# Two token-wise layers on one core: five parts of the instruction order regrouped around an in-order pipeline

## The reference

```python
# x: (2, 2048, 512), float32; per batch entry one expert of 5 and one category of 64
s0 = relu(x @ swi[0]) @ swo[0];  s1 = relu(x @ swi[1]) @ swo[1]     # 512 -> 2048 -> 512
eo = relu(x @ wi[type_label]) @ wo[type_label]
gate_in = concatenate([eo[:, 0], s0[:, 0], s1[:, 0]])               # first token only
w = softmax(relu(gate_in @ g1) @ g2)                                # 3 weights per batch entry
x = x + eo * w[0] + s0 * w[1] + s1 * w[2]
x = x + (x @ W[category] + b[category])
```

## Time and profile before

| | before |
|---|---|
| median of 3 runs | 2095.21 us (2089.08 to 2104.32) |
| profiled execution | 2096.13 us, span 2094.4 us |
| mean granted PE clock | 0.972 |
| PE busy | 1976.0 us (94% of the span), 8504 matmuls |
| DVE, ACT, POOL busy | 1258.6 (60%), 972.5 (46%), 857.7 us (41%) |
| chain that ended last | PE 84%, DMA 5%, issue 5%, DVE 4% |

### The profile page before, as it was taken

The page is one execution under the profiler, slowest core; times in us unless marked ns, Lnnn a source line. Parts: engine busy times, 40 slices in busy tenths (PEclk is TensorE's granted clock), DMA queues, the critical chain, the costliest instruction groups (busy, mean ns, idle before and its releaser), DMA issues.

```text
span 2094.4 us, 24883 instructions
## 1 busy us (share of the span) xinstructions
PE 1976.0 (94%) x8504; PEld 1618.5 (77%) x8504; DVE 1258.6 (60%) x1186; ACT 972.5 (46%) x1441; POOL 857.7 (41%) x607
## 2 busy tenths in 40 slices
PE   7999999888999898999899999988979989989998
PEld 5778777676788787888788888877868878878886
DVE  6778787778655454545644554576774645455545
ACT  5655755555553343334443444455554533334432
POOL 5767757557222232233422222365653222323233
PEclk8999999999999999999999999999999999999999
DMA  5666657656686575556686676576657756656653
GB/s 216 237 239 265 244 221 276 249 198 241 226 258 211 174 233 179 183 190 198 201 263 192 204 228 199 196 268 229 241 198 261 241 189 211 209 165 194 197 166 121
DMA packets 187024, 450.98 MB, mean 215 GB/s; under 512 B 16916, under 2 KB 57876, under 8 KB 180500
## 3 DMA queue, kind: packets, MB, share of 16 engines
q1 hardware_dynamic: 186900, 449.39, 63.4%
HBM read 308.81 MB, written 140.51 MB: 215 GB/s over the span
## 4 chain that ended last, share of the span: by engine, by line
PE 84%; DMA 5%; issue 5%; DVE 4%; ACT 1%; POOL 1%; SPq 0%; POOLq 0%; ACTq 0%; DVEq 0%
PE rps L1250 40%; PE ups L1250 40%; PE aps L1250 3%; DMA PDR<-in_L_cond_wo_dram 2%; DMA MB<-sums_kept 1%; DVE WD L953 1%; DMA XT<-in_x_dram 1%; DMA G1c<-in_L_cond_g_dram 1%; DVE WU L946 1%; DVE ACC L980 1%; DVE HL L963 1%; DVE XL L937 0%; POOL XT L660 0%; DMA PDR<-in_L_cond_swo_dram 0%; DVE gacc L1027 0%
## 5 line engine op out<-in xcount | busy, mean ns | idle before, releaser
L1250 PE MATMUL ups<-XH,WU 128*128 128x512 f32 x2688 | 901.0, 396 | 69.1 <-DVE HT L1002 25.7
L1250 PE MATMUL rps<-HH,WD 128*128 128x512 f32 x2688 | 898.5, 396 | 43.4 <-issue 42.5
L610 POOL TENSOR_TENSOR HT<-hid 128x512 f32<-128x512 f32 x192 | 267.4, 1393 | 1026.2 <-PE rps L1250 884.6
L1250 PEld LDWEIGHTS ups<-XH,WU 128*128 128x128 f32 x2688 | 513.3, 191 | 187.7 <-DVE HT L1002 27.4
L1250 PEld LDWEIGHTS rps<-HH,WD 128*128 128x128 f32 x2688 | 514.6, 191 | 159.4 <-issue 49.4
L1250 PE MATMUL rps<-HL,WD 128*128 128x512 f32 x1344 | 531.1, 395 | 0.0
L1250 PE MATMUL ups<-XL,WU 128*128 128x512 f32 x1344 | 530.3, 395 | 0.0
L963 DVE TENSOR_TENSOR HL<-HT,HH 128x1024 fp32r<-128x1024 f32 x240 | 305.9, 1294 | 47.7 <-POOL HT L610 35.0
L983 DVE SCALAR_TENSOR_TENSOR ACC<-rps,gw,ACC 128x1024 f32<-128x1024 f32 x129 | 165.4, 1283 | 277.7 <-PE rps L1250 277.7
L1250 PEld LDWEIGHTS rps<-HL,WD 128*128 128x128 f32 x1344 | 257.7, 192 | 53.8
L1250 PEld LDWEIGHTS ups<-XL,WU 128*128 128x128 f32 x1344 | 256.8, 191 | 52.7
(11 more groups left out here) (102 smaller groups left out, 1476.4 us busy)
## 6 DMA issues: line engine op xcount, KB each, us to landing
WU<-wu_kept SPq DMA_DIRECT2D x448, 256.0 KB, 3.2
WD<-wd_kept SPq DMA_DIRECT2D x224, 512.0 KB, 3.3
wd_kept<-WD SPq DMA_DIRECT2D x112, 512.0 KB, 2.9
wu_kept<-WU SPq DMA_DIRECT2D x32, 1024.0 KB, 5.8
wu_kept<-WU SPq DMA_DIRECT2D x32, 768.0 KB, 3.3
sums_kept<-ACC SPq DMA_DIRECT2D x28, 512.0 KB, 5.0
MB<-sums_kept SPq DMA_DIRECT2D x28, 512.0 KB, 5.6
PUR<-in_L_cond_swi_dram SPq DMA_DIRECT2D x16, 512.0 KB, 7.0
```

Source lines behind the costliest of these rows:

```text
L610: pool.tensor_tensor(dst, p, q, op).then_inc(s_T, 1)
L1250: ins = pe.matmul(dst, stationary[a], moving[c], start=start and j == 0, stop=stop and j == 2, skip_group_check=True)
```

## The change: what it does, and its diff

1. Weight requests: the down operand that was made after product 3 (product 0 of the next step) is made after product 4, together with product 1 (`made_after`). The raw down blocks of the next step are requested at i == 2, when product 5's low part is made; POOL's sums wait for product 6's low part.
2. Finishing of tokens: `mix(1, 2)` goes behind `second(6)`, and for odd c its load is requested at i == 5.
3. Ends of token blocks: `load_tokens(s + 1, 3)` is issued at the head of i == 5 instead of at i == 6; in the step `start` (rel 11) the low parts of token sums 2 and 3 come ahead of `hidden_low(d, 6)`.
4. Gate sums: the four operations of networks 0 and 1 are placed one by one in `second(1)` to `second(4)` of steps rel 8 and rel 9; those of the expert two by two in `second(0)` and `second(1)` of the gating step. The rest of the gate moves back by about two groups on PE, ACT and DVE. The second load of g1 is requested at i == 6.
5. First token sums: `XT` 4 and `XT` 5 of super 0 are made by POOL, beside DVE; their count moves to a semaphore of its own, and token sum semaphores are split in two. Super 0's low parts are awaited in the order in which they are made, and `up_low(0, 1)` comes before that of token block 2.
6. Hidden sums of half b: POOL makes HT 5 before HT 4, so HL 1 and HL 2 wait for three sums, not four.

The diff, without the hunks that only renumber semaphore counts:

```diff
+def made_after(m, i):
...
+    if i < 0:
+        m, i = m - 1, i + PRODUCTS
+    e = down_of(m, i) + WD_SLOTS
+    made = {PRODUCTS - WD_SLOTS: [], PRODUCTS - WD_SLOTS + 1: [e - 1, e]}.get(i, [e])
+    return [k for k in made if k >= 0 and prepared(k // PRODUCTS)]
...
+def x_low_count(s, i):
+    return PRODUCTS * s + (i if s == 0 else X_LO.index(i)) + 1
...
-s_xT = sem("token_sums")
+s_xT = sem("token_sums_T3_T2")
+s_xU = sem("token_sums_T1_T4")
...
         if PREP[N] >= 1:
-            sp.wait_ge(s_wld, PRODUCTS * PREP[N])
+            sp.wait_ge(s_wld, PRODUCTS * PREP[N] - 1)
+            sp.wait_ge(s_Sd, 4 * PREP[N])
...
         for i in range(PRODUCTS):
+            if i == 5 and m >= 0 and rel == STEPS_SUPER - 2 and s < SUPERS - 1:
+                load_tokens(s + 1, 3)
...
                         spill(d, j)
-            if e - 1 >= 0 and prepared((e - 1) // PRODUCTS):
-                keep_down((e - 1) // PRODUCTS, (e - 1) % PRODUCTS)
-            if i == 3 and prepared(N) and N > 0:
+            for k in made_after(m, i - 1):
+                keep_down(k // PRODUCTS, k % PRODUCTS)
+            if i == 2 and prepared(N) and N > 0:
...
                     if ms % 2 == 0:
-                        if stage == 0 and i in (2, 6):
+                        if stage == 0 and i == (5 if c % 2 else 2):
...
                             mix_tokens(ms, c + 1)
-                if s % 2 == 0 and i == 2:
-                    if rel == 7:
-                        load_g1(s // 2, 0)
-                    if rel == 8:
-                        load_g1(s // 2, 1)
+                if s % 2 == 0 and i == 2 and rel == 7:
+                    load_g1(s // 2, 0)
+                if s % 2 == 0 and i == 6 and rel == 8:
+                    load_g1(s // 2, 1)
...
                         load_tokens(s + 1, j)
-                if rel == STEPS_SUPER - 2 and i == 6 and s < SUPERS - 1:
-                    load_tokens(s + 1, 3)
...
         eng.wait_ge(s_xs[0], 16 * (s + 1))
-        eng.wait_ge(s_xT, 4 * s + 1)
+        eng.wait_ge(s_xT, 2 * s + 1)
...
     elif which == 2:
+        eng.wait_ge(s_xs[0], 16 * (s + 1))
+        eng.wait_ge(s_xs[1], 16 * (s + 1))
...
         eng.wait_ge(s_xs[3], 16 * (s + 1))
-        eng.wait_ge(s_xT, 4 * s + 2)
+        eng.wait_ge(s_xT, 2 * s + 2)
         dst, p, q, op = XT[:, 5, :], XT[:, 3, :], XT[:, 2, :], ALU.subtract
-    eng.tensor_tensor(dst, p, q, op).then_inc(s_xT, 1)
...
-x_from = [(XS, 0, 0, 0), (XT, 1, 1, 2), (XT, 2, 2, 4), (XT, 3, 0, 4), (XT, 4, 3, 0), (XT, 5, 4, 0), (XS, 2, 0, 0)]
+    eng.tensor_tensor(dst, p, q, op).then_inc(s_xT if which < 2 else s_xU, 1)
...
+none = (None, 0)
+x_from = [(XS, 0, none, none), (XT, 1, (s_xT, 1), (s_xT, 2)), (XT, 2, (s_xT, 2), (s_xU, 2)),
+          (XT, 3, none, (s_xU, 2)), (XT, 4, (s_xU, 1), none), (XT, 5, (s_xU, 2), none), (XS, 2, none, none)]
...
         pool.wait_ge(s_pd, 16 * (PREP[N] + 1))
+        if PREP[N] > 0:
+            pool.wait_ge(s_wld, PRODUCTS * PREP[N])
...
     up_sums(0)
+    token_sum(pool, 0, 2)
+    token_sum(pool, 0, 3)
...
         if d >= 0:
-            for which in range(4):
+            for which in (0, 1, 3, 2):
...
             act.wait_ge(s_up, PRODUCTS * (2 * STEPS_SUPER * s - 1) + i + 1)
-        t, slot, sums, _ = x_from[i]
-        if sums:
-            act.wait_ge(s_xT, 4 * s + sums)
+        t, slot, (made, count), _ = x_from[i]
+        if count:
+            act.wait_ge(made, 2 * s + count)
...
         if N > 0:
-            act.wait_ge(s_T, 8 * (N - 1) + 4 * half + 3)
+            act.wait_ge(s_T, 8 * (N - 1) + 5 * half + 3)
...
             else:
-                act.wait_ge(s_T, 8 * N + 4 + {3: 1, 2: 2, 4: 3, 5: 4}[i])
+                act.wait_ge(s_T, 8 * N + 4 + {3: 1, 2: 2, 5: 3, 4: 4}[i])
...
                 begin_sum(d, i)
-            e = down_of(m, i) + WD_SLOTS
-            if e >= 0 and prepared(e // PRODUCTS):
+            for e in made_after(m, i):
...
             chain(a)
-        if gating:
-            act.wait_ge(s_gps, 2 * (s // 2) + 1)
-            act.activation(gt[:, :], aps[:, 0:KD], ACT.Relu).then_inc(s_grelu, 1)
...
         second(2)
...
         second(2)
-        if gating:
-            act.wait_ge(s_gch, 2 * (s // 2) + 2)
-            act.activation(gexp[:, :], aps[:, 0:NETS], ACT.Exp,
...
         second(3)
+        if gating:
+            act.wait_ge(s_gps, 2 * (s // 2) + 1)
+            act.activation(gt[:, :], aps[:, 0:KD], ACT.Relu).then_inc(s_grelu, 1)
...
             relu_12(b)
+        if gating:
+            act.wait_ge(s_gch, 2 * (s // 2) + 2)
+            act.activation(gexp[:, :], aps[:, 0:NETS], ACT.Exp,
+                           bias=nmax[:, 0:1], accum_out=gsum[:, 0:1]).then_inc(s_gexp, 1)
+        if more:
...
         dve.wait_ge(s_xhi, PRODUCTS * s + X_HI.index(i) + 1)
-        t, slot, _, after = x_from[i]
-        if after:
-            dve.wait_ge(s_xT, 4 * s + after)
+        t, slot, _, (read, count) = x_from[i]
+        if count:
+            dve.wait_ge(read, 2 * s + count)
...
         dve.wait_ge(s_hhi, PRODUCTS * N + HI_ORDER.index(i) + 1)
-        after = {1: 8, 2: 8, 3: 6}
+        after = {1: 7, 2: 7, 3: 6}
...
-    def gate_partial(b, net):
+    def gate_partial(b, net, j):
...
-        for j in range(KD):
...
     token_low(0, 1)
-    token_sum(dve, 0, 2)
-    token_sum(dve, 0, 3)
-    token_low(0, 2)
...
                 add_sum(d, i)
-            e = down_of(m, i) + WD_SLOTS
-            if e >= 0 and prepared(e // PRODUCTS):
+            for e in made_after(m, i):
                 down_low(e // PRODUCTS, e % PRODUCTS)
+            if gating and i < 2:
+                gate_partial(s // 2, 2, 2 * i)
+                gate_partial(s // 2, 2, 2 * i + 1)
+            if m >= 0 and s % 2 == 0 and rel in (8, 9) and 1 <= i <= KD:
+                gate_partial(s // 2, rel - 8, i - 1)
...
             first_token(super_of(d - 1) // 2, net_of(d - 1))
-        if gating:
-            gate_partial(s // 2, 2)
         if m == -1:
-            for i in (3, 4, 5, 6):
+            for i in (2, 3, 4, 5, 6):
                 token_low(0, i)
-        if d >= 0:
-            hidden_low(d, 6)
...
             token_low(s + 1, 3)
+        if d >= 0:
+            hidden_low(d, 6)
...
         second(0)
-        if gating:
-            gate_terms(s // 2)
...
         second(2)
-        if gating:
-            gate_max(s // 2)
...
             up_low(b, 1)
+        second(3)
         if gating:
-            gate_weights(s // 2)
-        second(3)
+            gate_terms(s // 2)
...
         second(5)
-        mix(1, 2)
+        if gating:
+            gate_max(s // 2)
...
         second(6)
-        if m >= 0 and s % 2 == 0:
-            if rel == 7:
-                gate_partial(s // 2, 0)
-            if rel == 8:
-                gate_partial(s // 2, 1)
+        mix(1, 2)
+        if gating:
+            gate_weights(s // 2)
...
         if n % (2 * STEPS_SUPER) == 0:
-            pe.wait_ge(s_xlo, PRODUCTS * super_of(N) + X_LO.index(i) + 1)
+            pe.wait_ge(s_xlo, x_low_count(super_of(N), i))
...
                 down(d, i)
-            if gating and i == 0:
+            if gating and i == 2:
                 gate_hidden(m // (2 * STEPS_SUPER))
-            if gating and i == 2:
+            if gating and i == 4:
...
```

More of the change, by code:

```diff
@@ L876, in _ @@
                 second(2)
-                if gating:
-                    act.wait_ge(s_gch, 2 * (s // 2) + 2)
-                    act.activation(gexp[:, :], aps[:, 0:NETS], ACT.Exp,
-                                   bias=nmax[:, 0:1], accum_out=gsum[:, 0:1]).then_inc(s_gexp, 1)
                 if more:
@@ L1017, in gate_partial @@
                 G = G1c if net == 2 else G1
-                for j in range(KD):
-                    if k + j > 0:
-                        dve.wait_ge(s_gpart, k + j)
-                    if net == 0 and j == 0:
-                        if b > 0:
-                            dve.wait_ge(s_gps, 2 * b)
-                        dve.tensor_scalar(gacc[:, :], G[:, j, :], yv[:, net, j:j + 1], None,
-                                          ALU.mult).then_inc(s_gpart, 1)
-                    else:
-                        dve.scalar_tensor_tensor(out=gacc[:, :], in0=G[:, j, :], scalar=yv[:, net, j:j + 1],
-                                                 in1=gacc[:, :], op0=ALU.mult, op1=ALU.add).then_inc(s_gpart, 1)
+                if k + j > 0:
+                    dve.wait_ge(s_gpart, k + j)
+                if net == 0 and j == 0:
+                    if b > 0:
+                        dve.wait_ge(s_gps, 2 * b)
+                    dve.tensor_scalar(gacc[:, :], G[:, j, :], yv[:, net, j:j + 1], None,
+                                      ALU.mult).then_inc(s_gpart, 1)
+                else:
+                    dve.scalar_tensor_tensor(out=gacc[:, :], in0=G[:, j, :], scalar=yv[:, net, j:j + 1],
+                                             in1=gacc[:, :], op0=ALU.mult, op1=ALU.add).then_inc(s_gpart, 1)
```

## The result

The changed kernel takes 2044.82 us (median of 4 runs, 2041.07 to 2044.93), the kernel before 2094.21 in the same comparison. The ratio is 0.9757, with a 95% interval of 0.9733 to 0.9780. The forecast was 2021 us, with a range of 1994 to 2048: right in direction and inside the range, but 24 us short of the size, two thirds of the 75 us foretold.

The account below looks back on a forecast made before the run. PE was 84% of the chain of waits, so only its idle or slow time could be won. Terms 36 + 8 + 28 + 2 + 3 - 2 = 75 us off 2096.1 gave 2021 us, range 1994 to 2048.

Parts of the forecast that it names:

- What bounds the kernel: Whole span: PE is 84% of the chain of waits, and its losses sit in a few places.
- Finishing of tokens: Odd mixing slices: all four waits for block_21, 25.7 us, and their slow blocks go, 36 us saved; bounds 0 and 37.
- The rival in which the wait moves to the head of the step: Mixing: MB lands late and DVE waits at its step's head, half of the 36 us stay, 2039 us; chance 0.07.
- Gate sums: Around steps rel 7 to 9: spreading gate operations saves 7.5 us per expert stretch; the gating steps save 2 together.
- Weight requests: Prepared steps: earlier request saves 3 us per expert stretch, less 2.7 for the second low part; shared-network steps save 3.
- Ends of token blocks: Starts of supers: earlier fourth token block and reordered low parts save 8 us at super 2, 6 each at the others.
- First token sums: Kernel start: DVE sheds two operations but POOL takes 2.40 us for one, 2 us lost; between 1.4 gained and 2.5 lost.
- Hidden sums: HL 1 waits for one POOL sum less but DVE comes later anyhow: 0, except under 1 us at the end.
- The prepared steps give nothing back: Rival: DVE and POOL are the chain in prepared steps, so moving work among them gains nothing; 2052 us, chance 0.13.
- The slower rival: Twelve prepared steps: two low parts together delay block_22(b), PE stops mid-pair then runs slowly, 78 us lost; 2130 us, chance 0.03.
- Those for "right": No block_21 or PDR waits; 2 to 3 us gaps in steps 8, 9; 3 to 4 at supers 1, 3, none at 2.
- those for "wrong": DVE waits for MB; down product 1 waits 5 us; gaps mid-prepared-step at up products; 62 to 385 loses above 30 us.

Follow-up runs that it names:

- e4: The kernel before with the mixing part alone (mix(1, 2) behind second(6), its load at i == 5 for odd c): 2062.18 us, ratio 0.9854.
- e5: The kernel before with the gate operations of networks 0 and 1 alone spread out, second g1 load at i == 6, gating step as before: 2081.9 us.
- e3: The changed kernel with the gate operations of networks 0 and 1 in second(0) to second(3), one group earlier: 2037.17 us, ratio 0.9724.
- e9: The changed kernel with the whole weight part undone: product 0 made after product 3, raw down blocks requested at i == 3: 2038.98 us, ratio 0.9726.
- e1: The changed kernel with product 0 of the next down operand made after product 3 again, early request kept: 2021.68 us, ratio 0.9651.
- e6: The changed kernel with the fourth token block requested at i == 6 again, order of low parts as changed: 2049.15 us, ratio 0.9789.
- e12: e10 with HL 6 ahead of both token low parts at the start of a super, as in the kernel before: 2013.14 us, ratio 0.9621.
- e10: The changed kernel with the edits of e1 and e3, first token sums on VectorE, next super's first three token blocks requested at i == 0: 2009.9 us.
- e7: The changed kernel with GpSimd's hidden sums in the order of before, HL 1 and HL 2 waiting for all four: 2044.96 us, ratio 0.9769.

## Why the prediction was right or wrong

*What bounds the kernel.* Right. The path of the difference adds up to the spans' 51.3 us, at the places named; what was off are the prices.

*Finishing of tokens: 36 us.* Right in mechanism, and nearly in size: 32.5 alone (e4). The rest came back before down products. The rival in which the wait moves to the head of the step falls, since VectorE does not wait for MB.

*Gate sums: 7.5 us for each expert stretch and 2 for the gating steps.* The mechanism was right, the size too high: 10.9 us for the two stretches (e5) in place of 15. The term that was mis-sized is the operation in `second(4)`, 1.1 us and a slow block. It made PE wait for `block_22` as well, and moving it away gives 7.7 us by the medians and 3.9 between the profiled executions (e3). The gating step's own 2 us were not measured alone.

*Weight requests: 3 + 6 us won by the request and the shared steps, less 5.4 for the second low part.* Here a step failed in kind and not only in size. "I take 0.68, since the neighbouring one in the same place has it" is the sentence: one such operation in that place had 0.68, but a second right behind it meets GpSimd's next sum. The pair takes 2.37 us, so the moved part costs 1.7, the dear end of the bounds. On top of it steps 1 to 7 then all sit at a gap of 1.6 to 2.1 us. The pair cost 23.1 us; the whole part lost 5.8 us where the forecast had 3.6 won, inside its bounds. The request I had priced too low in turn: 17.3 us (e9 to e1), since without the pair it also brings the shared steps to their short gap and to full clock. Behind that stands a misreading of the earlier trace rows: I put the gap of 2.08 us at step 4 down to the first token's operation. But step 2, which has no such operation, had the same gap. Here is its chain in the kernel before, and then in e1:

```profile
136.19 2.10 issue
138.29 4.56 PE rps L1250 x12
```

```profile
138.94 0.86 issue
139.81 3.00 PE rps L1267 x12
```

e9, which differs from e1 in the request alone, has 1.98 us and 4.58 there, and step 4 itself has 1.10 us in e1. So the long gap came from the late request, and the first token's operation costs a few tenths; why only every second step had it stays open. Had the change kept the request alone, it would have reached 2021.7 us, the number of the forecast; that is chance, as two errors of the forecast cancel there.

*Ends of token blocks: 8 + 12 us.* Mis-sized, and by more than any other term. The request alone is worth 4.3 us (e6), and the order of low parts 3.2 us (e12 against e10), together some 12 us less than forecast. The traces agree: the gaps before up product 2 and down product 1 at the three starts are 18.4 us before and 12.4 in the changed kernel. At super 2 the gap of 5.4 us before up product 2 went, but 2.8 us of gap came before down product 1, where HL 6 and HL 1 now stand behind two token low parts; I had not asked what would be late next there. At supers 1 and 3 GpSimd's chain of sums set the time, as stated, and PE also waited for `block_22` behind the pair in the step before (2.4 and 3.5 us).

*First token sums: 2 us lost.* 2.8 by the medians, within the noise, and 2.4 by the traces. The page "SBUF — State Buffer" of the Trainium skill, section "Who interferes with whom", has the engine that starts first keep the shared port for its whole instruction. The trace agrees for the first of the two sums, behind which the low part took 2.55 us; the second found VectorE with one operation that had started first (14.13 against 14.17 us), and idle after it, and the loss was half of what two full blocks would have been.

*Hidden sums: 0.* Right (e7).

*The rivals.* "The prepared steps give nothing back" had 2052 us, which is 7 us from the measured time where the forecast is 24 off, and for the shared steps it described what the changed kernel did (1324 matmuls for 1326). As a rule it is false: e1 shows that they give back as soon as the order is right, and its premise, that VectorE and GpSimd are the limit however they are arranged, falls. The slower rival named the right mechanism, PE stopping within the pair behind two low parts, at 1.5 to 3.5 us and in six steps instead of 6.5 us in twelve; e1, without the pair, takes 8.9 us off these waits, and e3, with the gate operations a group earlier, 5.8.

*The signs.* Those for "right" came: no wait for `block_21`, none of ScalarE for PDR, gaps of 2.1 and 1.7 us in steps 8 and 9, and 2.95, 0.3 and 3.1 us at the starts of supers. But so did one of those for "wrong", the gaps at up products in the middle of prepared steps, and it pointed at the pair and the gate operation ahead of `block_22`.

The parts measured alone are 32.5, 10.9, 4.3, 3.2, -5.8 and -2.8, 42 us in all against the measured 49. They were taken in different surroundings and need not add.

## What to carry to other kernels

In an in-order engine a moved operation costs what it takes at its new place, beside the neighbours it has there: take the dear end of an operation's durations unless the row of that very place, with the other engine's work beside it, shows the cheap one. A request can be issued earlier without moving its first use; test the two edits apart. And when a wait goes, look up who is next in line on the same engine, and which other request now goes out at the same moment.

## What the runs showed that I had not expected

A gap of the same length is not always followed by slow matmuls. The two gaps of 2.03 us above were followed by a block in 3.00 and one in 4.55 us. The stretches of these blocks in the changed kernel (the last figures are granted clock, DMA share and GB/s):

```profile
303.00:309.60 6.60, 4.60 (x21) 3.48 (x20) 6.60 (x6) 6.60 (x11) 6.46 (x5) 1.00 0.74 233
309.60:314.20 4.60, 4.57 (x13) 3.71 (x14) 4.60 (x4) 1.12 (x3) 3.25 (x3) 0.63 0.54 215
146.50:149.50 3.00, 2.99 (x13) 2.49 (x14) 3.00 (x3) 0.87 (x3) 2.92 (x3) 1.00 0.40 161
```

After the one gap the granted clock was 0.63 over 4.6 us, a mixture of 1.2 and 2.4 GHz, though it had been 1.00 in the 6.6 us ahead; after the other it was 1.00. Against an undisturbed block of 2.72 us the price of a 2 us gap is then 2.3 or 3.9 us. Of the eight gaps in steps 1 to 8 of the changed kernel (1.6 to 2.1 us) three were followed by a slow block, and in e6 and e7 it was not the same steps, so a mean weighted by such a count is the honest term of a sum. At gaps of 0.9 to 1.1 us no block of e1's shared steps was slow, and the granted clock of that stretch was 1.00.
